# Layer 3's third slot group in half the slots, twice over the partitions, multiplied in pairs of half-height matmuls

## The reference, cut to what matters

```python
XW = X @ W                                   # 2048 x 128
s_col = XW @ a[0, :f];  s_row = XW @ a[0, f:]
Z1 = leaky_relu(s_row[:, None] + s_col[None, :], 0.01)
den = exp(Z1)
num = A @ den                                # 2048 x 2048 x 2048, A has 2 edges in a row on average
att = where(num != 0, den / where(num != 0, num, 1.0), 0.0)
H = A @ (att @ XW)
x = x + H
```

## Time and profile before

| | us |
|---|---|
| median of 3 runs | 700.52 (699.16 to 700.79) |
| the profiled execution | 699.03 |
| its span in the trace | 697.3 |
| PE busy in the span | 582.2 |
| DVE busy | 507.3 |
| ACT busy | 251.4 |
| POOL busy | 201.1 |

### The profile page before, as it was taken

The page is one execution under the profiler, slowest core; times in us unless marked ns, Lnnn a source line. Parts: engine busy times, 40 slices in busy tenths (PEclk is TensorE's granted clock), DMA queues, the critical chain, the costliest instruction groups (busy, mean ns, idle before and its releaser), DMA issues.

```text
span 697.3 us, 15068 instructions
## 1 busy us (share of the span) xinstructions
PE 582.2 (83%) x5740; PEld 542.4 (78%) x5740; DVE 507.3 (73%) x921; ACT 251.4 (36%) x397; POOL 201.1 (29%) x144
## 2 busy tenths in 40 slices
PE   0788589999903996898885699999999999999797
PEld 0677589999802653697873599999999999999797
DVE  3753498888295466265857689999999999999711
ACT  2699011111103223565551143333333333333363
POOL 1119000000020012253512044444444444444541
PEclk9995699999755999898998699999999999999999
DMA  8693111111000000000000000000000000000001
GB/s 282 270 374 137 37 47 47 42 35 45 0 1 0 1 1 0 0 2 0 2 0 4 1 2 2 2 0 0 0 0 0 0 0 0 0 0 2 0 17 45
DMA packets 8355, 24.37 MB, mean 35 GB/s; under 512 B 688, under 2 KB 3696, under 8 KB 6256
## 3 DMA queue, kind: packets, MB, share of 16 engines
q1 hardware_dynamic: 7328, 23.10, 9.1%
q10 hardware_dynamic: 976, 0.59, 0.6%
HBM read 22.61 MB, written 1.08 MB: 34 GB/s over the span
## 4 chain that ended last, share of the span: by engine, by line
PE 27%; DVE 24%; issue 16%; DVEq 1%; ACT 1%; POOL 1%; ACTq 0%; POOLq 0%
PE bank L1085 10%; PE bank L1226 7%; PE bank L1063 6%; DVE denc L1722 5%; DVE tc L1740 4%; DVE yc L1747 4%; DVE h L1338 2%; PE bank L1236 2%; DVE G L1607 2%; PE bank L1115 1%; DVE stats L1292 1%; PE bank L1207 1%; DVE e L1630 1%; POOL rstd L526 1%; DVE mv L1295 0%
## 5 line engine op out<-in xcount | busy, mean ns | idle before, releaser
L1226 PE MATMUL bank<-ATc,denc 128*128 128x128 f32 x1536 | 185.7, 279 | 15.2 <-ACT ATc L857 8.4
L1226 PEld LDWEIGHTS bank<-ATc,denc 128*128 128x128 f32 x1536 | 179.2, 194 | 17.2 <-issue 16.6
L600 POOL TENSOR_TENSOR dTc<-dTc,yc 128x512 f32<-128x512 f32 x64 | 112.9, 1764 | 163.7 <-ACT yc L851 111.8
L1085 PE MATMUL bank<-pcs,Ar 128*128 128x256 f32 x768 | 94.4, 286 | 7.2 <-DVEq L1324 3.7
L1085 PEld LDWEIGHTS bank<-pcs,Ar 128*128 128x128 f32 x768 | 93.2, 195 | 8.6 <-DVEq L1324 4.5
L849 ACT ACTIVATE yc<-bank 128x512 f32<-128x512 f32 x64 | 38.2, 597 | 164.0 <-PE bank L1226 164.0
L1722 DVE TENSOR_SCALAR denc<-cB,rc 128x2048 f32<-128x2048 f32 x48 | 84.9, 1773 | 0.3 <-DVE rc L1714 0.3
L458 POOL TENSOR_TENSOR rstd<-var,power 128x4 f32<-128x4 f32 x12 | 12.2, 1013 | 208.3 <-DVE var L1297 208.3
L1023 PE MATMUL bank<-whp,G 128*128 128x136 bf16 x768 | 63.8, 227 | 8.9 <-DVE G L1516 8.9
L1236 PE MATMUL bank<-XW,yc 128*128 128x128 f32 x512 | 67.5, 275 | 1.8 <-DVE yc L1747 1.8
L1063 PE MATMUL bank<-pcs,A 128*128 128x385 bf16 x256 | 44.4, 335 | 28.7 <-DVEq L1317 28.7
(11 more groups left out here) (194 smaller groups left out, 731.9 us busy)
## 6 DMA issues: line engine op xcount, KB each, us to landing
a<-in_adj SPq DMA_DIRECT2D x16, 1024.0 KB, 6.1
rows<-tau SPq DMA_DIRECT2D x16, 256.0 KB, 3.1
out<-X SPq DMA_DIRECT2D x4, 256.0 KB, 2.2
W<-in_L_gnn_W ACTq DMA_DIRECT2D x1, 192.0 KB, 7.0
attB<-in_L_gnn_att_weight ACTq DMA_DIRECT2D x1, 128.0 KB, 5.9
a3B<-in_L_gnn_a ACTq DMA_DIRECT2D x1, 128.0 KB, 8.6
W<-in_L_gnn_weight ACTq DMA_DIRECT2D x1, 64.0 KB, 1.9
W<-in_L_gnn_W ACTq DMA_DIRECT2D x1, 64.0 KB, 7.6
```

The source lines that it names most:

```text
L600: nc.gpsimd.tensor_tensor(own, own, yc[b][c][:, :], ALU.mult).then_inc(yd_ready, 1)
L1085: last = nc.tensor.matmul(bank[t % 2][:, 0:2 * D], Ar[t % 4][:, kt, :], pieces[:, kt, :], start=kt == 0, stop=kt == T - 1)
L1226: last = nc.tensor.matmul(bank[c][:, P * k:P * k + P], denc[b][:, part, j0:j0 + P], ATc3[b][:, part, :], start=part == 0, stop=part == NC - 1)
```

## The change

The groups become 6, 7 and 3 column tiles. The third, of 3 tiles, has at most 63 slots: a matmul adds 64 to its ranks (onesb times halfb, 128 x 0.5), so its slots are 65 to 127, and the limit of 127 stands. In layer 3, G3 of these three tiles compares with the upper half of iota twice, so that the same 64 rows (63 slots and the row for no edge) stand in partitions 0 to 63 and again in 64 to 127. The third group's table denw is then 128x1024: the lower partitions hold the columns of banks 0 and 2, the upper ones those of banks 1 and 3, from a row qBw that ACT builds beside qB3. PE does two banks at a time: 2 x 8 full-height matmuls for the first two groups, then 8 half-height ones that alternate between the two halves of the rows. one_hot3 becomes two instructions, and gather3 waits for both. In layer 0 only the cut of the groups is different, not the number of matmuls; one rank matmul is added.

```diff
-CHUNKS = ((0, 5), (5, 10), (10, 16))
+CHUNKS = ((0, 6), (6, 13), (13, 16))
+HP = P // 2
+JW = CHUNKS[2][0]
-        denc = [at(f"denc_{b}", 24 * b, [P, NC, N]) for b in range(2)]
+        denc = [at(f"denc_{b}", 24 * b, [P, NC - 1, N]) for b in range(2)]
+        denw = [at(f"denw_{b}", 24 * b + 16, [P, HALF]) for b in range(2)]
+        qBw = at("qBw", 199, [P, HALF])
...
+            nc.gpsimd.memset(halfb[:, :], 0.5).then_inc(const_ready, 1)
...
+                half, k = HP * (q % 2), BANK * (q // 2)
+                nc.scalar.activation(qBw[half:half + HP, k:k + BANK], bank[5][half:half + HP, :], ACT.Exp, scale=0.99)
                 nc.scalar.activation(qB3[:, js], bank[5][:, :], ACT.Exp, scale=0.99).then_inc(qt_ready, 1)
...
+            nc.tensor.matmul(ranks[:, :, JW:T], onesb[:, :], halfb[:, :].unsqueeze(2).to_broadcast([P, T, T - JW]),
+                             start=False, stop=False)
...
-            def num3(it, b, c):
+            def num3(it, b, p):
                 pe.wait_ge(denc_ready, 3 * it + 3)
                 pe.wait_ge(at3_ready, it + 3)
-                pe.wait_ge(t_ready, 4 * it + c + 1)
+                for c in (2 * p, 2 * p + 1):
+                    pe.wait_ge(t_ready, 4 * it + c + 1)
+                    for k in range(4):
+                        j0 = P * (4 * c + k)
+                        for part in range(NC - 1):
+                            nc.tensor.matmul(bank[c][:, P * k:P * k + P], denc[b][:, part, j0:j0 + P],
+                                             ATc3[b][:, part, :], start=k == 0 and part == 0, stop=False,
+                                             skip_group_check=True)
                 for k in range(4):
-                    j0 = P * (4 * c + k)
-                    for part in range(NC):
-                        last = nc.tensor.matmul(bank[c][:, P * k:P * k + P], denc[b][:, part, j0:j0 + P],
-                                                ATc3[b][:, part, :], start=part == 0, stop=part == NC - 1)
-                last.then_inc(num3_bank, 1)
+                    j0 = BANK * p + P * k
+                    for c in (2 * p, 2 * p + 1):
+                        rows = slice(HP * (c % 2), HP * (c % 2) + HP)
+                        last = nc.tensor.matmul(bank[c][:, P * k:P * k + P], denw[b][rows, j0:j0 + P],
+                                                ATc3[b][rows, NC - 1, :], start=False, stop=k == 3, skip_group_check=True)
+                        if k == 3:
+                            last.then_inc(num3_bank, 1)
...
-                for c in range(4):
-                    num3(it, b, c)
+                for p in range(2):
+                    num3(it, b, p)
                     if within(it, -1):
-                        u3(it - 1, 1 - b, c)
+                        u3(it - 1, 1 - b, 2 * p)
+                        u3(it - 1, 1 - b, 2 * p + 1)
...
-                nc.vector.tensor_tensor(G3[b][:, :, :], iota[:, :].unsqueeze(1).to_broadcast([P, T, P]), ...
+                nc.vector.tensor_tensor(G3[b][:, 0:JW, :], iota[:, :].unsqueeze(1).to_broadcast([P, JW, P]), ...
+                nc.vector.tensor_tensor(G3[b][:, JW:T, :].rearrange("p j (h s) -> p j h s", h=2),
+                                        iota[:, HP:P].unsqueeze(1).unsqueeze(1).to_broadcast([P, T - JW, 2, HP]), ...
...
-                nc.vector.tensor_scalar(denc[b][:, c, :], qB3[:, :], rc[b][:, c, 0:1], rc[b][:, c, 1:2],
+                den, row = (denc[b][:, c, :], qB3) if c < NC - 1 else (denw[b][:, :], qBw)
+                nc.vector.tensor_scalar(den, row[:, :], rc[b][:, c, 0:1], rc[b][:, c, 1:2],
                                         ALU.mult, ALU.max).then_inc(denc_ready, 1)
```

More of the change, by code:

```diff
@@ L157, in gnn_stack @@
         Eb = at("Eb", 176, [P, T, P], BF16)
-        x3 = at("x3", 202.75, [P, T, 3])
-        e3 = at("e3", 203, [P, T, 3])
+        x3 = at("x3", 203, [P, T, 3])
+        e3 = at("e3", 203.1875, [P, T, 3])
         ul3 = e3[:, :, 0:2]
         t3 = e3[:, :, 2]
[L162 to L167, removed]
+        cr2 = at("cr2", 203.375, [P, T, 2])
+        q3 = at("q3", 203.5, [P, T])
+        um3 = at("um3", 203.5625, [P, T])
+        rp = at("rp", 203.625, [P, T, 2, 3], BF16)
+        last3 = at("last3", 203.8125, [P, NC, 2])
+        rest2 = at("rest2", 203.84375, [P, T, 2])
         ATc3 = [at(f"ATc3_{b}", 196 + 1.5 * b, [P, NC, P]) for b in range(2)]
@@ L188, in gnn_stack @@
         iota = const("iota", [P, P], BF16)
+        halfb = const("halfb", [P, 1], BF16)
         rc = [const(f"rc_{b}", [P, NC, 2]) for b in range(2)]
@@ L447, in _ @@
             nc.gpsimd.memset(onesb[:, :], 1.0).then_inc(const_ready, 1)
-            pool.wait_ge(const_ready, 5)
+            nc.gpsimd.memset(halfb[:, :], 0.5).then_inc(const_ready, 1)
+            pool.wait_ge(const_ready, 6)
             nc.gpsimd.affine_select(out=ident[:, :], in_=ones[:, :], compare_op=ALU.is_equal, fill=0.0, base=0,
                                     pattern=[[-1, P]], channel_multiplier=1).then_inc(const_ready, 1)
-            pool.wait_ge(const_ready, 6)
+            pool.wait_ge(const_ready, 7)
             nc.gpsimd.tensor_copy(identb[:, :], ident[:, :]).then_inc(const_ready, 1)
@@ L893, in broadcast @@
                 nc.tensor.matmul(bank[4 + b][:, :], ones[:, :], dg[b][:, :], start=True, stop=True).then_inc(bc_bank, 1)
-            pe.wait_ge(const_ready, 7)
+            pe.wait_ge(const_ready, 8)
             def turn_tile(it):
@@ L1199, in gather3 @@
             def gather3(it, b):
-                pe.wait_ge(g3_ready, it + 1)
+                pe.wait_ge(g3_ready, 2 * it + 2)
                 pe.wait_ge(e3_copied, it + 1)
@@ L1606, in one_hot3 @@
                     apart(dve)
-                nc.vector.tensor_tensor(G3[b][:, :, :], iota[:, :].unsqueeze(1).to_broadcast([P, T, P]),
-                                        slotb[:, bass.ds(it, 1), :].rearrange("p o j -> p (o j)").unsqueeze(2)
-                                        .to_broadcast([P, T, P]), ALU.is_equal).then_inc(g3_ready, 1)
+                nc.vector.tensor_tensor(G3[b][:, 0:JW, :], iota[:, :].unsqueeze(1).to_broadcast([P, JW, P]),
+                                        slotb[:, bass.ds(it, 1), 0:JW].rearrange("p o j -> p (o j)").unsqueeze(2)
+                                        .to_broadcast([P, JW, P]), ALU.is_equal).then_inc(g3_ready, 1)
+                if not isinstance(it, int):
+                    apart(dve)
+                nc.vector.tensor_tensor(G3[b][:, JW:T, :].rearrange("p j (h s) -> p j h s", h=2),
+                                        iota[:, HP:P].unsqueeze(1).unsqueeze(1).to_broadcast([P, T - JW, 2, HP]),
+                                        slotb[:, bass.ds(it, 1), JW:T].rearrange("p o j -> p (o j)").unsqueeze(2)
+                                        .unsqueeze(3).to_broadcast([P, T - JW, 2, HP]), ALU.is_equal).then_inc(g3_ready, 1)
             one_hot3(0, 0)
```

## The result

The changed kernel takes 705.91 us (median of 5 runs, 702.24 to 707.97), the kernel before beside it 699.16 (median of 5, 696.12 to 700.79). The ratio is 1.0083, with a 95% interval from 1.0051 to 1.0115: slower by 0.5 to 1.2%. The forecast was 706.3 and slower.

What follows compares the result with a forecast made beforehand. DVE was taken to set layer 3's block pace. 12 x 0.42 = 5.0, plus 1.25 at the tail, less 0.53, gave +5.8 on the profiled 699.03: 704.8; with 1.5 for the median, 706.3 us, range 702 to 710.

Steps and rivals of the forecast that it cites:

- DVE sets the pace and PE follows: Layer 3's blocks: DVE sets the 16.57 us block, and PE, with 15.87 us of work, follows 0.7 us behind.
- DVE's own gain: DVE in a layer 3 block: halved third den3, less the cost of splitting one_hot3, saves 0.46 us a block.
- The order of products and pieces: Layer 3 block: POOL's products come in two pairs, the first entering between one_hot3's pieces; block 16.99 us, 0.42 longer.
- Pairs side by side: PE's half-height matmuls in num3: loads of the two halves run beside each other, 0.89 us a group instead of 1.79.
- A change of height: PE in num3: switching between full and half height costs 0.09 us, four a block; upper bound 0.34.
- The tail: End of layer 3: banks 2 and 3 come out together, so one inverse more stands on the path, +1.25 us.
- The halved den3 ahead of the first block: Start of layer 3's blocks: the halved den3 there gives back 0.53 us, once.
- The sum: Whole kernel: 5.0 us from the blocks, 1.25 at the tail, less 0.53 at the start, makes +5.8 us.
- the steady term: Layer 3's middle blocks: 12 blocks of full rhythm, each 0.42 us longer, make +5.0 us.
- Rival A: PE in layer 3: half-height loads come in turn and PE sets the pace; 697.1 us (692.8 to 709.1); chance 0.35.
- Rival B: Layer 3 blocks: products fall as before, so DVE keeps its 0.46 us a block; 695.7 us; chance 0.12.
- Rival C: PE, idling 2.5 us a block, loses its granted clock of 1.00; some 12 us per affected block, slower; chance 0.03.

Runs made afterwards that it cites:

- the small products: POOL's product takes only 16 of each bank's 512 columns, part of the computation left out: 677.40 us on the changed kernel, 696.18 on the kernel before.
- the bank-by-bank kernel: The changed kernel with num3 done bank by bank, so half-height matmuls form no pairs: 715.15 us, ratio 1.021.
- the run with late casts: The changed kernel, but POOL starts its two casts of layer 3's rows only when the last attention is made: 704.12 us, ratio 1.006.

## Why the prediction was right, step by step

- *DVE sets the pace and PE follows.* Shown by the small products: with the cover gone PE's saving appears in full (1.05 us a block), and with the products in place none of it does.
- *DVE's own gain, forecast 0.46.* The two kernels with the product on DVE differ by 16.31 - 15.84 = 0.47.
- *The order of products and pieces.* Forecast: two pairs, the first asking inside one_hot3's first piece and getting in between the pieces, the second pair lengthening refine and the halved den3. So it came, to the instruction. Bank 1's product has den3 at 2.2, as forecast. The block is 16.89 instead of 16.99, 0.31 more than before instead of 0.42. But the trace has eight such blocks where the forecast had twelve: 2.4 us instead of 5.0.
- *Pairs side by side.* Right: one load beside the other, as the Trainium skill, TensorEngine Tiling (Array Packing), section Key Properties, has it; 0.11 us a pair, 0.78 for eight starts.
- *A change of height, forecast 0.09.* Wrong by a factor of two: 0.20 from the loads, 0.19 from the bank-by-bank kernel. I took the one row of such a change; it was one row with 8 columns to multiply, and the upper bound 0.34 was almost as near. The other rule that the Trainium skill gives in that section, that a change of the mode drains TensorE, agrees with the dearer price, 0.20 us. PE's work is so 14.80 instead of 14.4, its idle time 2.09 instead of 2.5. (In the sum for it, 1.49 should be 1.51, which changes nothing.) Nothing of it reached the time, because PE is not on the path; a PE-bound kernel would have paid 0.4 us a block for this step.
- *The tail, forecast +1.25.* Wrong in size and in mechanism: +3.74 in the profiles. The step that failed put one more inverse on the path and took the rest of the tail as it stood. The last inverse ends 1.4 us earlier than before and is not on the path. DVE is: its split waits for POOL's late pair of products and the casts, the last refine ends 1.71 us later, and the last u3, at half the clock, takes 1.73 us more. The forecast had nothing for either.
- *The halved den3 ahead of the first block, -0.53.* Not to be told apart: the first interval between two own3 is 15.22 us in the changed kernel's trace, 16.61 before, but 16.67 in the run with late casts, whose code up to there is the same.
- *The sum.* That the forecast's +5.8 lies near the medians' +6.75 is in part luck. In the traces, which differ by 2.85, the steady term was too large (eight blocks longer, +2.4, five others shorter, -2.25) and the tail too small, and the stretch ahead of layer 3's first own3 differs by -1.09 for no reason that I know. Where the other 3.9 us of the medians lie no trace shows.
- *Rival A, PE's pace.* Out as a description of the changed kernel: the loads are not in turn. Sorted by half, where they nearly are, DVE was still last, 17.30 against the 15.5 that the rival gave DVE: the rival had the products miss refine and den3, and they did not.
- *Rival B, products at their old places.* It appears in single blocks: see the next point.
- *Rival C, the clock.* It came in small, with the opposite sign. Four times in layer 3's blocks the granted clock fell to 0.50, the lower level of 1.2 GHz. One such place, PE's timeline, the window, then DVE's timeline of the block behind it:

```profile
490.71 5.46 PE L1238 MATMUL bank<-ATc,denc 128*128 128x128 f32 x32 [2.13 <-DVE denw L1750]
```

```profile
492.10:495.50 3.40, 3.40 (x18) 3.40 (x18) 3.03 (x3) 0.00 (x0) 0.00 (x0) 0.50 0.00 0
```

```profile
496.48 1.89 DVE L1628 TENSOR_TENSOR G<-iota,slotb 128x1664 bf16<-128x1664 bf16 x1
498.28 0.55 DVE L1633 TENSOR_TENSOR G<-iota,slotb 128x384 bf16<-128x384 bf16 x1
498.75 2.32 DVE L1750 TENSOR_SCALAR denc<-cB,rc 128x2048 f32<-128x2048 f32 x1
```

PE takes 5.46 us for 32 records instead of 3.74, so bank 0's product asks 1.7 us later, behind the second piece, which keeps its 0.47. The block to the next one_hot3 is 512.96 - 496.48 = 16.48 us, shorter than its neighbours' 16.89; behind each of the four places the next block is shorter in this way (16.27 to 16.50). A slower PE made a faster block: it is the place of the products that counts, seen without any edit.

## What to carry to other kernels

Where two engines keep each other out, an engine's block is its own work plus what each foreign instruction lengthens, and only the order of starts tells which; write that order out to a tenth of a microsecond before a faster engine beside it is counted as a gain. A cheap instruction on an idle engine can be the dear one: in the changed kernel the four products were worth 3.47 us of DVE's time on POOL and 2.40 on DVE (in the kernel before 2.68 and 2.40, and there the move gained no time). And walk the tail with its own order, including the work of the next stage that starts there and the clock behind a long wait, instead of adding one latency to it.

## What the runs showed of the hardware

- Half-height f32 loads of the two row halves start within 0.01 us of each other, a pair every 0.11 us; sorted by half the same 16 records take 1.63 us instead of 1.09, so most of the gain came from alternating the halves in the program.
- A change between full and half height costs 0.20 us in either direction. Four of them take 0.8 us a block from the 1.8 that the pairs alone would save (2 x (1.79 - 0.89)); 1.05 was measured.
- In eight blocks of the changed kernel PE stood idle for 2.00 to 2.13 us; in three of them the granted clock fell to 0.50 (458.0, 492.1, 608.2), in the other five it stayed at 1.00. The idle time alone, as far as these traces show, does not decide it.
- A product that POOL asks for during one of DVE's instructions gets in when that one ends, ahead of DVE's next (asked at 513.44, in at 514.76), and a second product behind it gets in ahead of the one after that: two DVE instructions in a row are lengthened, here by 1.09 and 0.95 us.
